# Attention with decayed scores: the score matmuls as three rounded passes over the whole array, and the next batch's query and key projection earlier

## The reference

```python
q = proj(query, Wk, bk); k = proj(key, Wk, bk); v = proj(values, Wv, bv)
scores = jnp.einsum('bhqd,bhkd->bhqk', q, k) / np.sqrt(dk)
scores_ = softmax(where(allow, scores, NEG)) * allow        # allow: lower triangle
distcum = cumsum(scores_); disttotal = sum(scores_)
dist_scores = sqrt(clip((disttotal - distcum) * |i - j|, 0, None))
total_effect = clip(exp(dist_scores * -softplus(gammas)), 1e-5, 1e5)
attn = softmax(where(allow, scores * total_effect, NEG))
query2 = concat(attn @ v) @ Wo.T + bo
x = layer_norm(query + query2)
x = layer_norm(x + relu(x @ W1.T + b1) @ W2.T + b2)
```

## Time and profile before

| | |
|---|---|
| runs, median (lowest to highest) | 1489.0 us (1486.66 to 1491.96) |
| the profiled execution, its time | 1490.92 us |
| its span | 1489.1 us |
| mean granted TensorE clock | 0.988 |
| TensorE busy | 1432.6 us (96%) |
| VectorE busy | 1084.9 us (73%) |
| ScalarE busy | 1024.4 us (69%) |
| GpSimd busy | 158.5 us (11%) |

### The profile page before, as it was taken

How to read it: one execution, slowest core, us unless ns; L and a number is a source line. 1 busy time by engine, 2 the same in 40 slices (tenths; PEclk the granted TensorE clock), 3 DMA queues, 4 the chain that set the end, 5 groups by cost and what they waited for, 6 DMA issues and landing times.

```text
span 1489.1 us, 32758 instructions
## 1 busy us (share of the span) xinstructions
PE 1432.6 (96%) x12140; PEld 1157.6 (78%) x12140; DVE 1084.9 (73%) x3780; ACT 1024.4 (69%) x2626; POOL 158.5 (11%) x180
## 2 busy tenths in 40 slices
PE   5797899999999999999999999999999999999998
PEld 4455688888888888888888878888888888888887
DVE  6997868787787767777776867767777776867533
ACT  4774768777677768767676767768677676776622
POOL 4213010101001010100101010010100101010100
PEclk9899999999999999999999999999999999999999
DMA  8775657676666566665665666566665666667965
GB/s 282 269 253 205 236 215 278 222 259 226 236 257 219 216 219 245 203 233 206 224 244 193 246 204 219 217 219 241 219 230 200 219 220 220 245 216 254 334 258 189
DMA packets 89142, 345.90 MB, mean 232 GB/s; under 512 B 17624, under 2 KB 35800, under 8 KB 56344
## 3 DMA queue, kind: packets, MB, share of 16 engines
q1 hardware_dynamic: 76544, 335.06, 63.2%
q0 software_dynamic: 10208, 7.94, 1.7%
q10 hardware_dynamic: 2232, 0.81, 0.2%
HBM read 316.16 MB, written 27.53 MB: 231 GB/s over the span
## 4 chain that ended last, share of the span: by engine, by line
PE 85%; DVE 5%; issue 4%; DMA 4%; ACT 1%; SPq 1%; POOL 0%; ACTq 0%; DVEq 0%; POOLq 0%
PE bank L228 22%; PE bank L229 21%; PE bank L230 21%; PE bank L530 9%; PE bank L544 6%; PE bank L564 2%; DMA zi_out<-z 2%; PE bank L581 1%; DVE w_sb L1391 1%; PE bank L505 1%; DMA zi_row<-zi_out 1%; DVE w_sb L1379 1%; DMA wk_raw<-wk 1%; PE bank L567 1%; DVE w_ring L1359 1%
## 5 line engine op out<-in xcount | busy, mean ns | idle before, releaser
L228 PE MATMUL bank<-xt_hi,w_ring 128*128 128x256 f32 x1008 | 294.7, 292 | 5.8 <-issue 2.8
L229 PE MATMUL bank<-xt_lo,w_ring 128*128 128x256 f32 x1008 | 285.1, 283 | 0.0
L230 PE MATMUL bank<-xt_hi,w_ring 128*128 128x256 f32 x1008 | 284.9, 283 | 0.0
L1367 DVE CUSTOM_DVE_ANT_0 s_sb<-bank,mask 128x256 f32<-128x256 f32 (+7 forms) x512 | 129.9, 302 | 181.7 <-PE bank L530 181.1
L974 ACT COPY pt_sb<-bank 128x512 f32<-128x512 f32 x192 | 112.0, 583 | 170.5 <-PE bank L544 169.0
L964 ACT ACTIVATE p_sb<-w_sb,nm 128x32 f32<-128x32 f32 (+7 forms) x512 | 205.3, 404 | 3.6 <-DVE nm L1406 3.6
L228 PEld LDWEIGHTS bank<-xt_hi,w_ring 128*128 128x128 f32 x1008 | 192.7, 191 | 17.3 <-issue 10.6
L228 PE MATMUL bank<-w_ring,h_hi 128*128 128x512 f32 x504 | 202.1, 401 | 0.9 <-DVE h_lo L1469 0.9
L230 PE MATMUL bank<-w_ring,h_lo 128*128 128x512 f32 x504 | 197.7, 392 | 0.0
L229 PE MATMUL bank<-w_ring,h_hi 128*128 128x512 f32 x504 | 197.7, 392 | 0.0
L229 PEld LDWEIGHTS bank<-xt_lo,w_ring 128*128 128x128 f32 x1008 | 192.9, 191 | 0.8
(11 more groups left out here) (144 smaller groups left out, 2685.2 us busy)
## 6 DMA issues: line engine op xcount, KB each, us to landing
w_ring<-w_split SPq DMA_DIRECT2D x248, 1024.0 KB, 5.1
w_split<-w_ring SPq DMA_DIRECT2D x32, 512.0 KB, 5.3
xc_raw<-x_t SPq DMA_DIRECT2D x16, 512.0 KB, 3.9
xc_raw<-ctx_t SPq DMA_DIRECT2D x16, 512.0 KB, 5.1
u_sb<-x_rows SPq DMA_DIRECT2D x16, 512.0 KB, 6.4
ring_raw<-w SPq DMA_DIRECT2D x32, 256.0 KB, 5.7
out<-rows SPq DMA_DIRECT2D x15, 512.0 KB, 9.3
zi_row<-zi_out POOLq DMA_DIRECT2D x58, 128.0 KB, 4.9
```

Source lines behind the costliest of these rows:

```text
L228: nc.tensor.matmul(dst, a_hi, b_hi, start=start, stop=False)
L229: nc.tensor.matmul(dst, a_hi, b_lo, start=False, stop=False)
L230: return nc.tensor.matmul(dst, a_lo, b_hi, start=False, stop=stop)
L1367: m = nc.vector.tensor_tensor_reduce(out=s_sb[:, c % 2, W_AT[b] + 1:W_AT[b] + 1 + WIDTH[b]], in0=s_bank[n % 2][:, at:at + WIDTH[b]], in1=m ...
```

## The change

**Scores.** From quad 9 on (`PLAIN` = 9; 55 of the 64 quads) a block of scores is three matmuls over the whole array instead of four small ones. The stationary operand is a 128x128 tile in which the 32 queries of head h stand in rows 32h to 32h + 31 and columns 32h to 32h + 31, with zeros elsewhere, and the moving operand is the keys of all four heads, 128 rows. Both are split in a rounded high part and a rounded remainder: `q_hi`, `q_lo` (8 blocks x 128 columns) and `k_hi`, `k_lo` (`k_parts`). GpSimd writes the zeros once in the prologue (two fills of 1024 columns).

**Copies.** ScalarE's `qk_copy` becomes five instructions: four of 32 partitions x 256 for `q_hi` and one of 128 x 256 for `k_hi`. VectorE gets a new step, `qk_low`, of five instructions of the same sizes for `q_lo` and `k_lo`, which also read `pj_bank`. It raises `qk_lo_ok`, and from quad 9 on TensorE waits for that (`copied(n)`) where it waited for `qk_ok`: before the first scores of the quad and before whatever it writes to `pj_bank` next. The parts have one buffer where `qk_sb` had two; `qk_copy` waits until the scores of the quad before are done.

**Order.** On VectorE `running_sums` is cut in two after `gz`; `qk_low` of the next quad stands between the halves. `concat_low(i - 1, 3)` moves behind the sums of quad 1. On TensorE `queries_keys(i + 1, 0)` goes ahead of `hidden(i - 1, 1)`, and `values(i, 1)` behind `add_hidden(i - 2, 2)`; on ScalarE `qk_copy(i + 1, 0)` goes ahead of the first half of `second_exp(i, 2)`, and `value_rows(i, 1)` behind `concat_high(i - 1, 2)`.

```diff
@@ scores, TensorE
+            def copied(n):
+                if n < PLAIN:
+                    pe.wait_ge(qk_ok, n + 1)
+                else:
+                    pe.wait_ge(qk_lo_ok, n - PLAIN + 1)
...
                 for b in S_GROUPS[g]:
+                    if NQ * i + c >= PLAIN:
+                        q_parts = [q[:, b].rearrange("p h r -> p (h r)") for q in (q_hi, q_lo)]
+                        k_parts = [k[:, S - WIDTH[b]:S] for k in (k_hi, k_lo)]
+                        mm = three_passes(s_bank[n % 2][:, at:at + WIDTH[b]], *q_parts, *k_parts, True, True)
+                        at += WIDTH[b]
+                        continue
@@ step, TensorE
                 if ffn:
                     hidden(i - 2, 3)
+                    add_hidden(i - 2, 2)
                 if now and i not in AHEAD:
-                    pe.wait_ge(qk_ok, NQ * i + 2)
+                    copied(NQ * i + 1)
                     values(i, 1)
-                if ffn:
-                    add_hidden(i - 2, 2)
...
                 if last:
-                    pe.wait_ge(qk_ok, min(NQ * i + 3, NQ * B))
+                    copied(min(NQ * i + 2, NQ * B - 1))
                     project_rows(i - 1, 0)
...
                 if now:
                     attend(i, 1)
+                if ahead:
+                    copied(NQ * i + 3)
+                    queries_keys(i + 1, 0)
                 if last:
                     hidden(i - 1, 1)
-                if ahead:
-                    pe.wait_ge(qk_ok, NQ * i + 4)
-                    queries_keys(i + 1, 0)
-                if last:
                     add_hidden(i - 1, 0)
@@ qk_copy, ScalarE
+                n = NQ * i + c
+                if n >= PLAIN:
+                    act.wait_ge(s_mm, NS * n)
+                    if n == PLAIN:
+                        act.wait_ge(zeros_ok, 2)
+                    for h in range(HQ):
+                        on = slice(DK * h, DK * h + DK)
+                        nc.scalar.activation(q_hi[on, :, h], pj_bank[on, 0:S].rearrange("p (b r) -> p b r", r=R),
+                                             ACT.Identity, bias=bk_col[on, c:c + 1])
+                    nc.scalar.activation(k_hi, pj_bank[:, S:2 * S],
+                                         ACT.Identity, bias=bk_col[:, c:c + 1]).then_inc(qk_ok, 1)
+                    return
@@ VectorE
+            def qk_low(i, c):
+                n = NQ * i + c
+                if n >= PLAIN:
+                    dve.wait_ge(qk_ok, n + 1)
+                    for h in range(HQ):
+                        on = slice(DK * h, DK * h + DK)
+                        nc.vector.scalar_tensor_tensor(q_lo[on, :, h],
+                                                       pj_bank[on, 0:S].rearrange("p (b r) -> p b r", r=R),
+                                                       bk_col[on, c:c + 1], q_hi[on, :, h].bitcast(F32),
+                                                       ALU.add, ALU.subtract)
+                    nc.vector.scalar_tensor_tensor(k_lo, pj_bank[:, S:2 * S], bk_col[:, c:c + 1],
+                                                   k_hi.bitcast(F32),
+                                                   ALU.add, ALU.subtract).then_inc(qk_lo_ok, 1)
@@ step, VectorE
                 if last:
                     concat(i - 1, 3)
+                if now:
+                    running_sums(i, 1)
+                if last:
                     concat_low(i - 1, 3)
                 if now:
-                    running_sums(i, 1)
+                    qk_low(i, 2)
+                    weighed_sums(i, 1)
...
                 if now:
                     running_sums(i, 2)
+                    qk_low(i, 3)
+                    weighed_sums(i, 2)
                     concat(i, 0)
```

More of the change, by code:

```diff
@@ L92, in build @@
         xt_hi, xt_lo = (tensor(n, [P, KT, S], F32R) for n in ("xt_hi", "xt_lo"))
+        k_parts = tensor("k_parts", [P, 2, 2, S], F32R)
+        k_hi, k_lo = k_parts[:, 0, 0], k_parts[:, 0, 1]
         ident = tensor("ident", [P, P])
@@ L102, in build @@
         xc_hi = tensor("xc_hi", [P, KT, 2, S], F32R)
-        qk_sb = tensor("qk_sb", [P, 2, 2, S])
+        q_hi, q_lo = (tensor(n, [P, NB, HQ, R], F32R) for n in ("q_hi", "q_lo"))
         s_sb = tensor("s_sb", [P, 2, QW])
@@ L160, in build @@
         qk_ok = sem("qk_ok")
+        qk_lo_ok = sem("qk_lo_ok")
+        zeros_ok = sem("zeros_ok")
         v_ok = sem("v_ok")
@@ L653, in first @@
                 scores(0, 1, 2)
-                pe.wait_ge(qk_ok, 2)
+                copied(1)
                 queries_keys(0, 2)
@@ L663, in first @@
                 scores(0, 2, 2)
-                pe.wait_ge(qk_ok, 3)
+                copied(2)
                 queries_keys(0, 3)
@@ L687, in first @@
                 scores(1, 0, 2)
-                pe.wait_ge(qk_ok, 5)
+                copied(4)
                 queries_keys(1, 1)
@@ L1184, in step @@
                     deviation2(i - 3)
+                if last:
+                    concat_high(i - 1, 2)
                 if now and i not in AHEAD:
                     value_rows(i, 1)
-                if last:
-                    concat_high(i - 1, 2)
                 if last:
@@ L1253, in step @@
                     features(i - 1, 1)
-                if now:
-                    second_exp(i, 2, 0)
                 if ahead:
@@ L1258, in step @@
                 if now:
+                    second_exp(i, 2, 0)
                     second_exp(i, 2, 1)
@@ L1508, in first @@
                 running_sums(0, 0)
+                weighed_sums(0, 0)
                 splits(0)
@@ L1514, in first @@
                 running_sums(0, 1)
+                weighed_sums(0, 1)
                 splits(1)
@@ L1520, in first @@
                 running_sums(0, 2)
+                weighed_sums(0, 2)
                 splits(2)
@@ L1529, in first @@
                 running_sums(0, 3)
+                weighed_sums(0, 3)
                 splits(3)
@@ L1538, in first @@
                 running_sums(1, 0)
+                weighed_sums(1, 0)
                 splits(4)
@@ L1546, in first @@
                 running_sums(1, 1)
+                weighed_sums(1, 1)
                 concat(0, 3)
@@ L1561, in first @@
                 running_sums(1, 2)
+                weighed_sums(1, 2)
                 splits(6)
@@ L1573, in first @@
                 running_sums(1, 3)
+                weighed_sums(1, 3)
                 concat(1, 1)
@@ L1595, in step @@
                     running_sums(i, 0)
+                    qk_low(i, 1)
+                    weighed_sums(i, 0)
                 if last:
@@ L1671, in step @@
                     running_sums(i, 3)
+                if ahead:
+                    qk_low(i + 1, 0)
+                if now:
+                    weighed_sums(i, 3)
                 if now and not ahead:
@@ L1761, in _ @@
             assert made[0] == CONSTS
+            for q in (q_hi, q_lo):
+                nc.gpsimd.tensor_scalar(q[:].rearrange("p b h r -> p (b h r)"), carry[:, 0:NB * P], 0.0, None,
+                                        ALU.mult).then_inc(zeros_ok, 1)
             def split_high(at):
```

27 lines of the change are left out of this document (15 added, 12 removed).

## The result

The changed kernel is slower: 1559.3 us as the median (1558.0 to 1560.8), against 1488.2 for the kernel before on the same chip. The ratio is 1.047 (1.0455 to 1.0489). The spans of the two profiled executions are 1558.0 and 1489.1 us, 68.9 apart. The forecast was 1532 with a range up to 1558, so the sign and the places were right, and the time lies just above the range. A few executions (of the kernel before 1759 and 1996 us, of e2 1992, of e8 4521) were slow as a whole; every time and ratio here is of the others.

What follows compares the result with a forecast made beforehand. TensorE's own queue was taken to bound the kernel. The span of 1489.1 us plus 38 of waits, less 5 gained by the passes, plus 10 of half clock gave 1532 in span, and 1532 as median time; range 1478 to 1558.

Steps and rivals of the forecast that it cites:

- What bounds the kernel: In the batches TensorE's own queue is the time; any new wait of TensorE that recurs every batch adds in full.
- The scores on TensorE: Score groups: loads of about 0.11 us pace short matmuls, taken as 0.112 each; a quad falls from 2.79 to 2.71 us.
- a sign of being wrong: Score matmuls on TensorE: the prediction called itself wrong if short ones start closer than 0.08 us.
- the first rival: Score passes on TensorE cost their columns alone, 1.72 us a quad, gaining 59 us in all: 1478 us; chance 0.16.
- The gain of the passes: Scores of 55 quads on TensorE: 0.08 us saved per quad, 4 us, taken as 5 with first transposes spared.
- The two waits: TensorE waits for `qk_low` ahead of quad 3's scores, 2.05 us, and ahead of `project_rows`, 0.65 us, 14 times each.
- The waits in all: TensorE's new waits for `qk_low` over 14 batches: 14 x 2.7 = 38 us, from 29 to 46.
- The end of a batch: Ahead of the next batch's `values(i + 1, 0)`: `qk_low` ends slightly later, but TensorE is later too; nothing counted.
- The clock: Behind waits of 2 us TensorE sometimes runs 3 us at half clock, losing 1.5 us: 7 of 14, 10 us, 0 to 21.
- The range: Whole kernel's time with 0.8 probability: 1478 to 1558 us, covering nearly all the forecast's span and parts of rivals.
- the forecast's own case: Whole kernel if the main forecast holds, given 0.68: 1532 us, with ends of 1503 and 1561.

Runs made afterwards that it cites:

- e2: Changed kernel, but VectorE writes only the keys' remainder, one instruction of `qk_low` instead of five; the queries' remainder stays zero: 1498.3 us, ratio 1.0066.
- e8: Changed kernel with its copies, remainders, waits and order, but scores again four plain 32x32 matmuls per block, remainders waited for and unused: 1556.0 us, ratio 1.0462.
- e3: Changed kernel, but VectorE writes the remainders of the keys and of two heads' queries only, three instructions instead of five: 1501.3 us, ratio 1.0084.
- e5: Changed kernel with `queries_keys(i + 1, 0)` back behind `hidden(i - 1, 1)` on TensorE, and its copy on ScalarE moved back too: 1586.2 us, ratio 1.0654.
- e6: Changed kernel with TensorE reordered: quad 3's scores later, behind other work, and quad 0's first transposes ahead of `project_rows`; nothing added: 1524.2 us, ratio 1.0243.
- e4: Changed kernel plus nine unused 512-column matmuls on TensorE ahead of quad 3's first scores in batches 2 to 14: 1539.0 us, ratio 1.0339.

## Why the prediction was wrong, step by step

- **What bounds the kernel** was right: every new wait of TensorE came through in full. Waits, half clock and TensorE's own work make up the 66.5 us between the second and the fifteenth `project_rows`.
- **The scores on TensorE.** That loads of 0.11 us set the pace of short matmuls was right, but not that no matmul starts sooner: the second one of 96 columns starts 0.04 behind the first, closer than the 0.08 that the prediction gave as a sign of being wrong. What counts is the mean over a group, and it is 0.105, a little under the 0.112 taken. That refutes the first rival, columns alone, which has 0.072 for a matmul (it decides from 0.080 on; the 0.077 in the prediction is a slip). A pace of 81 ns, which the Trainium skill ("TensorE: Matmul & The Clock Gate", section "Back-to-back issue gap") states for 128 columns, isn't kept either: single starts are as close, but those of 128 columns are 0.10 apart on average, and the 24 of a quad 0.105. The gain of the passes was forecast at 5 us, and beside plain scores with the same waits it is 6 (e8). Against the kernel before only 1 is left of it, since TensorE's own work grows with the waits (the 6 us between e3 and the change). That term was not in the forecast, though the earlier trace rows had shown the 0.1 us behind an unhidden load.
- **The two waits** stand where they were forecast, in every batch, and are 2.23 and 0.79 instead of 2.05 and 0.65. The price was low: I took `qk_low` as two and a half pairs of the earlier trace rows, 2.1 us, where five instructions in a row start 0.49 apart and take 2.45. Also not seen: 1.2 to 2.3 us ahead of `project_rows` in three batches. In two the scan had waited 0.3 us for ScalarE's first exponential. In the longest, at 474.94, `concat` had waited for the DMA of `zi_row`:

```profile
468.46 0.63 DVE L1469 TENSOR_TENSOR cc_sb<-bank,zi_row 128x256 f32<-128x256 f32 x1 [3.21 <-DMA zi_row<-zi_out]
...
474.94 0.50 PE L237 MATMUL bank<-wo_hi,cc_hi 128*128 128x512 f32 x1 [2.30 <-DVE k_parts L1421]
```

   The waits in all: 46.9, where 38 (29 to 46) was said: above its upper end too.
- **The end of a batch** was forecast at nothing and is 0.19, 13 times. e5 shows that the move hides 2 us there, as said.
- **The clock is the step that failed.** The forecast took 7 of 14 waits at 1.5 us each, 10 us, at most 21. It was 10 of 14, and four of these stretches lasted 6.8 us, not 3.4, so that one of them costs 3.1 us and not 1.5. With the one behind `project_rows` that is 24 us. That a wait of 2 us can cost the clock was right; how often and how much was taken from a single case. The earlier trace rows had only one such wait in which the clock fell, and I took the 3 us that I had looked at as its length. The upper end of 21 was 14 times the cheapest fall, so it was no bound.
- **The range.** The upper end of the forecast's own case was 1561, which holds the result; its last 3 us were left out of the range, and the result was in them. Together 9 us too little for the waits, 14 too little for the clock and 4 too many for the gain make the 27 us between 1532 and 1559.

What stays open is what decides whether a wait of 2.2 us costs the clock: in the change 10 of 14 at quad 3 did, in e8 three of 14, and in e5 14 stretches stand against 27 such waits. Waits of 1.2 us cost it twice in 14 (e3), and e6, whose waits are 1.8 at most, never.

## What to carry to other kernels

Where TensorE's queue is the time, a new handoff is priced by the fixed work on the other engines from the last step that waits for TensorE up to the operand, less TensorE's own work in that stretch. Add up starts of instructions in a long run, not halves of a pair. Rounded matmuls over the whole array, each with its own load of 128 columns, came 0.11 us apart here because their loads did, so blocks of 32 to 224 columns gained little from being narrow. Waits of 2 us that came back each batch cost half as much again in clock here (24 us on 46.9), and TensorE's own work grew by 6 us with them as well (e3 against the change): first move independent work into them, and price what the engine that is late will be late for next (e6).

## What was not expected of the hardware

- Every stretch at half clock between 160 and 1450 us lasted 3.4 or 6.8 us, while TensorE was busy again. In the change the seven short ones began 0.6 to 1.5 us after the wait had ended, so the first instructions behind it still ran at full clock (686.79, full until 687.4 and half until 690.8), and the four long ones from 0.3 us before its end to 0.1 behind. In e8 two short ones began at the end of a wait or 0.35 before, so the begin alone doesn't settle the length. Matmuls whose result nobody reads, put into the wait, kept the clock full behind it in all 13 batches that had them, and gave 20 us back (e4).
- An instruction on 32 partitions takes as long as one on 128 with the same 256 elements each. Here are both of `qk_low`, by line (busy us, mean ns, idle before):

```profile
L1417 DVE SCALAR_TENSOR_TENSOR q_lo<-bank,bk_col,q_hi 32x256 fp32r<-32x256 f32 x220 | 105.5, 479 | 2.4
...
L1421 DVE SCALAR_TENSOR_TENSOR k_parts<-bank,bk_col,k_parts 128x256 fp32r<-128x256 f32 x55 | 26.6, 483 | 0.8
```
